# Index supply with three replica buffers and two staging buffers, and a reordered shift of batch 0, in a cross-attention and table-weight FFN kernel

## What is computed

```python
def attn(q, k, v):                  # 16 heads of 32
    p = softmax(einsum('bhqd,bhkd->bhqk', q, k) * HD ** -0.5)
    return einsum('bhqk,bhkd->bhqd', p, v)
q = head_norm(layernorm(x) @ Wq + bq)
k, v = head_norm(y[:, :-16] @ Wk + bk), y[:, :-16] @ Wv + bv
kd, vd = head_norm(y[:, -16:] @ Wkd + bkd), y[:, -16:] @ Wvd + bvd
x = x + (attn(q, k, v) + attn(q, kd, vd)) @ Wo + bo
gate, up, down = lut[gate_idx], lut[up_idx], lut[down_idx]   # 1376x512, 1376x512, 512x1376
n = layernorm(x)
x = x + (silu(n @ gate.T) * (n @ up.T)) @ down.T
```

## Time and profile before

| | us |
|---|---|
| median of three runs | 851.1 |
| profiled execution | 852.15 |
| its span | 850.0 |
| PE busy | 777.9 (92%) |
| DVE busy | 521.7 (61%) |
| ACT busy | 489.0 (58%) |
| POOL busy | 232.6 (27%) |

### The profile page before, as it was taken

How to read it: one execution, slowest core, us unless ns; L and a number is a source line. 1 busy time by engine, 2 the same in 40 slices (tenths; PEclk the granted TensorE clock), 3 DMA queues, 4 the chain that set the end, 5 groups by cost and what they waited for, 6 DMA issues and landing times.

```text
span 850.0 us, 14775 instructions
## 1 busy us (share of the span) xinstructions
PE 777.9 (92%) x5842; PEld 313.7 (37%) x5842; DVE 521.7 (61%) x1007; ACT 489.0 (58%) x993; POOL 232.6 (27%) x248
## 2 busy tenths in 40 slices
PE   3777666699999999999999999999999999999998
PEld 1332122222345333333454333324543332255445
DVE  7879899787685899321757993216579931053211
ACT  3577567677645788565357885652568856521100
POOL 6772210000057222100472222003732210013320
PEclk9987768799999999999999999999999999999999
DMA  7928844366521000122210001312100000000001
GB/s 242 263 96 245 241 142 110 82 159 155 137 53 35 1 1 1 51 62 50 69 46 1 1 1 34 79 38 75 27 1 1 1 26 26 26 25 1 0 13 38
DMA packets 72532, 56.50 MB, mean 66 GB/s; under 512 B 33232, under 2 KB 60624, under 8 KB 72464
## 3 DMA queue, kind: packets, MB, share of 16 engines
q1 hardware_dynamic: 72128, 55.31, 24.1%
q10 hardware_dynamic: 208, 0.26, 0.1%
q0 software_dynamic: 128, 0.00, 0.0%
HBM read 40.67 MB, written 8.45 MB: 58 GB/s over the span
## 4 chain that ended last, share of the span: by engine, by line
PE 67%; DVE 19%; ACT 4%; SPq 3%; DMA 2%; issue 2%; POOL 2%; DVEq 0%; POOLq 0%; ACTq 0%
PE ps L1339 49%; PE ps L1613 6%; DVE arena L890 5%; PE ps L1594 4%; DVE nmax L1145 3%; PE ps L1567 3%; DVE nmax L1146 3%; DMA arena<-idx 2%; PE ps L1390 2%; ACT ps L793 2%; SPq L368 2%; DVE nmax L1142 2%; DVE arena L897 2%; PE ps L1513 1%; PE ps L1600 1%
## 5 line engine op out<-in xcount | busy, mean ns | idle before, releaser
L1339 PE MATMUL ps<-arena,wf_hi 128*128 128x512 f16 (+2 forms) x736 | 211.1, 371 | 4.1 <-DVE arena L897 3.0
L793 ACT ACTIVATE ps<-ps,nmax 128x496 f32<-128x496 f32 x256 | 165.8, 649 | 26.9 <-DVE nmax L1145 26.9
L821 ACT ACTIVATE arena<-ps 128x1024 f32<-128x1024 f32 x128 | 124.2, 1024 | 72.7 <-PE ps L1600 72.6
L1339 PE MATMUL ps<-arena,wf_lo 128*128 128x512 f16 (+2 forms) x368 | 136.1, 370 | 0.0
L1339 PE MATMUL ps<-wf_hi,arena 128*128 128x512 f16 (+3 forms) x374 | 114.8, 368 | 0.0
L590 POOL TENSOR_TENSOR hrstd<-hvar,mhalf 128x16 f32<-128x16 f32 (+1 forms) x33 | 98.0, 2984 | 44.7 <-DVE hvar L994 44.5
L1339 PEld LDWEIGHTS ps<-arena,wf_hi 128*128 128x128 f16 (+1 forms) x736 | 69.4, 100 | 90.2 <-DVE arena L897 13.1
L1390 PE MATMUL ps<-arena,wf_lo 128*32 128x512 f16 (+1 forms) x1056 | 80.9, 444 | 22.4 <-ACT wf_lo L660 16.6
L890 DVE TENSOR_SCALAR arena<-arena,wf_lo 128x2048 f16<-128x2048 f16 (+1 forms) x132 | 89.8, 740 | 14.8 <-DMA arena<-idx 11.1
L566 POOL TENSOR_TENSOR xrstd<-xvar,mhalf 128x1 f32<-128x1 f32 x32 | 20.0, 624 | 249.7 <-DVE xvar L932 249.7
L1339 PE MATMUL ps<-wf_lo,arena 128*128 128x512 f16 (+3 forms) x187 | 68.5, 366 | 0.0
(11 more groups left out here) (137 smaller groups left out, 1060.4 us busy)
## 6 DMA issues: line engine op xcount, KB each, us to landing
arena<-idx SPq DMA_DIRECT2D x124, 128.0 KB, 2.9
arena<-in_x SPq DMA_DIRECT2D x32, 256.0 KB, 3.0
wf_lo<-in_idx SPq DMA_DIRECT2D x10, 512.0 KB, 6.4
idx<-wf_hi SPq DMA_DIRECT2D x10, 384.0 KB, 5.1
out<-arena SPq DMA_DIRECT2D x15, 256.0 KB, 2.1
wf_lo<-in_idx SPq DMA_DIRECT2D x11, 256.0 KB, 8.1
arena<-in_ctxT SPq DMA_DIRECT2D x4, 512.0 KB, 4.6
arena<-in_Wq SPq DMA_DIRECT2D x4, 256.0 KB, 5.8
```

Of the source, the lines that this page charges most:

```text
L793: last = act.activation(sc, sc, ACT.Exp, bias=nmax[:, 0, t, h:h + 1], accum_out=den[:, 0, t, h:h + 1])
L821: act.activation(probs[n_ % 2][:, 2 * p:2 * p + 2, :], ps[:, bank:bank + 2, :], ACT.Exp).then_inc(s["probs_set"], 1)
L1339: last = pe.matmul(dst, l, r, start=(first and i == 0), stop=(stop and i == len(todo) - 1))
```

## The change

- Replicas get three buffers (the third in `ctx_first`, free once the context is split), so `load_rep(c)` waits for `one_hot(c - 3)`. Staging buffers go from four to two.
- SP issues `load_rep(c)` first in each step c, then store k and load k + 2 at c = 2k - 1 only, so that blocks move until c = 19. Steps with x work move by one.
- POOL's cast of block k waits for the one-hots of 2k - 5 chunks where that is more than k - 1, and `lookup_out` waits only for the cast of the blocks whose staging it overwrites.
- Batch 0's shift: a quarter of `one_hot(15)` stays ahead of the extra keys' work, one goes ahead of the sum and two behind it; all four low halves of `Wo` come behind the copy (L1174). `look_up(15)` moves from the shift into the first slot of phase two, all later look-ups of phase two one slot on, and the last two (31 and 32) stand behind phase two.
- ACT's high half of `Wo` becomes four pieces in slots 4, 6, 8 and 10 of phase one.
- In phase two of batches 0 to 2, a tile's standardisation (L937) comes one slot later than its moments, and moments and split stand behind the slot's `one_hot` or feed-forward work.

```diff
@@ -31,7 +31,7 @@
...
 NJ, NR4 = 4, 4
-STAGES, EARLY = 4, 1
+STAGES, REPS = 2, 3
 QK_SCALE = float(HD) ** -0.5
@@ -61,7 +61,8 @@
...
 S_ONE = NU + 2
-S_SHIFT = S_ONE + NS
+S_SUM = S_ONE + NS
+S_SHIFT = S_SUM + 1
 S_TWO = S_SHIFT + 2
@@ -263,6 +264,7 @@
...
         ctx_first = cut(KC * S)
+        l_rep += [ctx_first.bitcast(F16)]
         ctx_dca = cut(KC * MD)
@@ -281,7 +283,8 @@
...
         i_at = c_at - STAGES * 2 * STEP
-        l_idx = [wf_lo[:, i_at + i * 2 * STEP:i_at + (i + 1) * 2 * STEP].bitcast(I32) for i in range(STAGES)]
+        idx_at = [i_at + (STAGES - 1 - i) * 2 * STEP for i in range(STAGES)]
+        l_idx = [wf_lo[:, at_:at_ + 2 * STEP].bitcast(I32) for at_ in idx_at]
         l_c = [wf_lo[:, c_at + i * P:c_at + (i + 1) * P].rearrange("p (q k) -> p q k", q=NJ) for i in range(2)]
@@ -360,12 +363,14 @@
...
                     sp.wait_ge(s[f"idx_out{c // 3}"], 16)
-                if c >= 2:
-                    sp.wait_ge(s["oh_set"], NJ * (c - 1))
+                if c >= REPS:
+                    sp.wait_ge(s["oh_set"], NJ * (c - REPS + 1))
+                elif c == REPS - 1:
+                    sp.wait_ge(s["cT_lo"], 1)
                 src = idx16[:, lo:hi].rearrange("(g k) n -> k g n", g=NR4)
                 for r in range(NR4):
-                    dst = l_rep[c % 2][r * 32:(r + 1) * 32, 0:NR4 * (hi - lo)].rearrange("p (g n) -> p g n", g=NR4)
-                    sp.dma_start(dst, src).then_inc(s[f"rep_in{c % 2}"], 16)
+                    dst = l_rep[c % REPS][r * 32:(r + 1) * 32, 0:NR4 * (hi - lo)].rearrange("p (g n) -> p g n", g=NR4)
+                    sp.dma_start(dst, src).then_inc(s[f"rep_in{c % REPS}"], 16)
 
@@ -389,8 +394,7 @@
...
                 load_idx(it)
-            for it in range(EARLY):
-                store_idx(it)
+            store_idx(0)
             load_rep(0)
@@ -407,20 +411,22 @@
...
 
-            next_x = {4: (0, 1), 21: (2,), 24: (3,)}
-            turn_x = {21: 0, 24: 1, 27: 2, 30: 3}
-            for c in range(2, NCH):
-                if EARLY + c - 2 < IT:
-                    store_idx(EARLY + c - 2)
-                if c == 2:
+            load_rep(2)
+            store_idx(1)
+            next_x = {4: (0, 1), 22: (2,), 25: (3,)}
+            turn_x = {22: 0, 25: 1, 28: 2, 31: 3}
+            for c in range(REPS, NCH):
+                load_rep(c)
+                if c == REPS:
                     dca_values((0, 0))
+                if c % 2 and (c + 1) // 2 < IT:
+                    store_idx((c + 1) // 2)
                 if c in turn_x:
...
                     load_x(t, tile_of(flat, xaddr(0, 1, t)), xs[t % 2])
-                load_rep(c)
 
@@ -533,7 +539,7 @@
...
                 elif it > 1:
-                    pool.wait_ge(s["oh_set"], NJ * (it - 1))
+                    pool.wait_ge(s["oh_set"], NJ * max(it - 1, 2 * it - 5))
                 pool.wait_ge(s[f"idx_in{it % STAGES}"], 32 * (it // STAGES + 1))
@@ -654,8 +660,9 @@
...
                 act.wait_ge(s["oh_used"], NJ * (c + 1))
-                if lo < i_at <= hi - 1 or (c == 0 and i_at == 0):
-                    act.wait_ge(s["idx_16"], IT)
+                for i, at_ in enumerate(idx_at):
+                    if lo < at_ + 2 * STEP and hi > at_:
+                        act.wait_ge(s["idx_16"], max(it + 1 for it in range(IT) if it % STAGES == i))
                 act.activation(wf_hi[:, lo:hi], ps[:, FB, 0:hi - lo], ACT.Copy)
@@ -839,15 +846,21 @@
...
             def prepare(slot):
-                if slot == S_ONE + 3:
+                if slot in (S_ONE + 4, S_ONE + 6, S_ONE + 8, S_ONE + 10):
+                    g = (slot - S_ONE) // 2 - 2
                     act.wait_ge(s["wo_in"], 16)
-                    act.activation(fl(wo[0]), st_o, ACT.Copy, scale=WS).then_inc(s["wo_hi"], 1)
-                for c in lookups_in(slot):
-                    if c:
-                        lookup_out(c - 1)
+                    act.activation(wo[0][:, g, :], st_o[:, g * D:(g + 1) * D], ACT.Copy, scale=WS).then_inc(s["wo_hi"], 1)
+                if S_ONE <= slot < S_SUM - 1:
+                    for c in lookups_in(slot):
+                        if c:
+                            lookup_out(c - 1)
+                elif slot >= S_SHIFT + 1:
+                    for c in lookups_in(slot):
+                        lookup_out(c - 2)
 
             core((0, 0), prepare, (0, 1), None)
-            lookup_out(NCH - 1)
+            for c in range(NCH - 2, NCH):
+                lookup_out(c)
 
@@ -877,17 +890,17 @@
...
 
-            def one_hot(c):
+            def one_hot(c, quarters=range(NJ)):
                 lo, hi = CHUNKS[c]
                 n_ = NR4 * (hi - lo)
-                dve.wait_ge(s[f"rep_in{c % 2}"], 16 * NR4 * (c // 2 + 1))
+                dve.wait_ge(s[f"rep_in{c % REPS}"], 16 * NR4 * (c // REPS + 1))
                 if c == 0:
...
                     dve.wait_ge(s["ps1"], T)
-                for q in range(NJ):
+                for q in quarters:
                     if c:
                         dve.wait_ge(s["oh_used"], NJ * (c - 1) + q + 1)
-                    dve.tensor_scalar(l_oh[q][:, 0:n_], l_rep[c % 2][:, 0:n_], l_j[:, q:q + 1], None, ALU.is_equal)\
+                    dve.tensor_scalar(l_oh[q][:, 0:n_], l_rep[c % REPS][:, 0:n_], l_j[:, q:q + 1], None, ALU.is_equal)\
                        .then_inc(s["oh_set"], 1)
@@ -1156,6 +1169,7 @@
...
                 dca_shift(T - 1)
+                between(S_SUM)
                 dca_sum(T - 1)
@@ -1182,12 +1196,14 @@
...
                         attn_lo(n_ // T - 1)
-                    if nxt is not None:
-                        if n_ in NORM_AT:
-                            norm(1, NORM_AT[n_], nxt)
-                        if n_ in TURN_AT:
-                            stage(1, TURN_AT[n_], nxt)
+                    if nxt is not None and n_ - 1 in NORM_AT:
+                        t = NORM_AT[n_ - 1]
+                        standardise(1, t, nxt, xs[t % 2], xs[t % 2])
                     between(S_TWO + n_)
+                    if nxt is not None and n_ in NORM_AT:
+                        moments(1, NORM_AT[n_], nxt, xs[NORM_AT[n_] % 2])
+                    if nxt is not None and n_ in TURN_AT:
+                        stage(1, TURN_AT[n_], nxt)
                 attn_lo(G - 1)
@@ -1290,12 +1306,16 @@
...
             def prepare(slot):
-                if slot in (S_SHIFT, S_SHIFT + 1):
-                    dve.wait_ge(s["wo_hi"], 1)
-                    for g in (0, 1) if slot == S_SHIFT else (2, 3):
+                if slot == S_SHIFT + 1:
+                    dve.wait_ge(s["wo_hi"], G)
+                    for g in range(G):
                         low(wo[1][:, g, :], st_o[:, g * D:(g + 1) * D], wo[0][:, g, :]).then_inc(s["wo_lo"], 1)
+                if slot == S_SUM:
+                    one_hot(NQ - 1, (1,))
+                if slot == S_SHIFT:
+                    one_hot(NQ - 1, (2, 3))
                 for c in lookups_in(slot):
-                    one_hot(c)
+                    one_hot(c, (0,) if c == NQ - 1 else range(NJ))
 
@@ -1627,10 +1647,13 @@
...
                 for c in lookups_in(slot):
-                    if c:
+                    if slot < S_SUM and c:
                         look_up(c - 1)
+                    elif slot >= S_TWO:
+                        look_up(c - 2)
 
             core((0, 0), prepare, (0, 1), None)
+            look_up(NCH - 2)
             look_up(NCH - 1)
```

4 lines of the change are left out of this document (2 added, 2 removed).

## The result

The changed kernel takes 836.02 us (median of 4 runs, 835.61 to 836.72), where the kernel before takes 850.7 us (848.22 to 851.44): a ratio of 0.9833, interval 0.9812 to 0.9855. The forecast was 837, with a range of 831 to 846. The profiled span fell from 850.0 to 834.3 us.

The account below looks back on a forecast made before the run. DVE was taken to bound phase one and PE phase two of batch 0; 852.15 - 7.3 - 4.5 - 4.0 + 1.4 = 837.75, on the runs' scale 836.7, said as 837, range 831 to 846.

Parts of the forecast that it names:

- Phase one: Batch 0, 60 to 151 us: replica, Wo and cast waits go, 8.3 us, less 1.0 kept back for PE's clock: 7.3.
- rival D: Casts throughout batch 0's DVE-bound stretch collide with DVE if blocks land late; three cost 4.4 us, 841; chance 0.03.
- the jam: Batch 0, 60 to 110 us: loading a block every step delays replicas; slower blocks and earlier loads remove all 4.7 us.
- The shift: Batch 0, from the last maxima to the second set of scores: reordering starts these about 4.5 us earlier; bounds 2.5 to 5.5.
- Phase two: Batch 0's PE-bound stretch up to the last value product: 61.5 us becomes 57.5, 4.0 less; bounds 0 to 5.5.
- Rival B: Batch 0's PE-bound stretch gains nothing: x work still touches on DVE, or SP's transposes delay replicas; 841; chance 0.13.
- The end: Behind batch 0's last value product, two look-ups instead of one: 5.6 us where 4.2 were, 1.4 us more.
- The allowances: Reserves held back from the gains: 1.0 us for PE's lower clock, 1.5 us for replicas and DVE in PE-bound slots.
- rival A: In batch 0, all reserves come back (1.0 + 1.5, and a bit around the logarithm): 834 us; chance 0.12.
- C: PE's lower clock makes PE the bound of batch 0's first stretch: 7 us lost, 844; chance 0.08.
- E: Stores and block loads on SP's queue delay replicas over 2 us in eight steps: 16 us lost, 853; chance 0.04.

Follow-up runs that it names:

- the repeat: The changed kernel measured again, unaltered, beside the other experiments: 836.01 us in the first group, 835.21 us in the third.
- the best experiment: Changed kernel with PE's wait for the last copy-outs and Wo's low half moved behind batch 1's first two products: 832.95 us.

## Why the prediction was right

- **Phase one**: 7.3 us predicted, 7.9 measured. All waits went, as said, and of the 1.0 us held back for the clock nothing was needed; the clock rose. Instead 1.7 us went to the collisions of rival D, which I had set at 0.03. D's condition (blocks that land late) was not what brought them: of the three casts that collide, two start on time, released by a one-hot. Of the six casts after 85 us three lie over an extra-key instruction. The held instruction ends 0.27 or 0.28 us after the end of its cast each time (85.76 + 1.47 = 87.23 and 86.72 + 0.79 = 87.51 for the first), and so do all 28 held instructions of the fourteen traces. The Trainium skill, SBUF — State Buffer, section "Who interferes with whom", describes one engine held for the whole instruction of the other; here 0.42 us became 0.79 and 1.37, and 0.42 again when the cast moved away. Without collisions phase one is 78.59 us (casts later), 9.5 less than before, where the terms added up to 8.3. So a gain that I had counted too small and a loss that I had left out nearly cancelled, which was luck.
- **Why replicas were late** was half right. I had put it down to the jam that blocks at every step make. With blocks at every step and 270 GB/s, three buffers had no wait; with two buffers, slow blocks and replicas first in SP's order phase one had none either. Each of the two cures alone is enough in phase one, and the slow blocks, beside three buffers, cost 1.1 us by their later casts. The number came out right because I had taken the whole wait off, whichever cured it.
- **The shift**: 4.5 predicted, 5.0 to the second scores. With its order undone the stretch is 15.67 us, as before, so the order is the cause. Of its 5.2 us against the repeat 3.8 are left at batch 1's first product, mostly because the end is longer with it. The half microsecond over the forecast is the look-up's: the one behind the first scores took 3.06 us, not the 3.60 that I had counted. The drain of about 1380 ns that the Trainium skill gives in ScalarE: Activation LUTs, "What ACT_TABLE_LOAD costs", isn't there: in the changed kernel the load ran from 142.87 for 1.28 us, the activation ahead of it ended at 142.86, and the next instruction of ACT started at 144.17.
- **Phase two**: 4.0 predicted with 1.5 held back; from the second scores to the end of the last value product are 207.90 - 151.33 = 56.6 us, where 61.5 were, so 4.9. From scores to scores thirteen slots take 3.70 us, one 4.3. Rival B is out. Its first reason (moments next to standardisation) cost nothing beside the lag. Its second (SP at a transpose while a replica is due) was real, as two buffers show with 4.18 us, and the third buffer covers it. What I didn't see is that buffer and order need each other: the buffer alone brings phase two from 61.5 us to 60.4, the new order with two buffers leaves it at 61.6, and both give 56.6. DVE's replica waits, 6.4 us before and 11.4 with two buffers, don't show this, since undisturbed slots take 3.70 us in both kernels and the stretch is as long; the larger sum took the place of other waits, and 4.18 of it lie behind phase two.
- **The end**: 1.4 us more predicted, 1.9 measured (gaps of 0.97 and 1.19, the look-up at 2.39 instead of 1.91 us). This was the one term against the change, and the best experiment takes 1.0 to 1.4 us of it back.
- The allowances together (1.0 and 1.5) were the distance to rival A. The measured 836.0 lies between the two. Rivals C and E stayed out: the clock didn't bound phase one, and no replica was late in a step with a block.

What stays open: how the 13 to 15 us of the whole split between buffer and order. Undoing one at a time gives 9.9 and 2.5 (and 1 for Wo), adding the buffer alone gives 3; the parts need each other, and no split of the sum holds for both directions. Which part of the order the buffer needs in phase two, the lag of the look-ups, the x work or the place of replicas on SP, isn't shown: with the buffer, undoing the lag cost 0.75 us and undoing the x work nothing.

## What to carry to other kernels

The sum of an engine's waits for one thing is not what curing them is worth. Take one cause away and another wait can fill its place, so a buffer and a better order are to be priced together, on the length of the stage (here 61.5 us, 60.4 and 61.6 with one of them, 56.6 with both). On a queue that issues other work too, what a buffer is worth shows in how late the issues come and not in bandwidth (here 3.0 us for the last chunk, at a share of 0.58). A change that spreads an engine's work over a longer time also spreads what that work collides with. And when the end of a stage is pulled in, look at what the next stage loads, and at what releases that load: work that you move later can hold it back.

## What the runs showed of the hardware

- A share of 0.96 of the DMA engines, 270 GB/s, made no engine wait for a replica that had two steps of time.
- In the jam one issue of a block load held SP for 3.50 us (before) and 2.90 (a block every step), where it takes 0.70 to 0.83 in the changed kernel.
- The look-up of 32 products behind the first scores took 2.79, 3.06 and 3.60 us in three profiles of one kernel, and 2.13 to 3.60 over all kernels, between its times at the upper clock (1.91) and the lower (3.60), though the transposes and scores ahead of it are the same and take the same time. What decides when the clock comes back there stays open; it moves the end by up to 0.8 us from run to run.
- Beside casts of the same kernel the three extra-key instructions took 0.79, 1.37 and 0.78 us in one profile, and 0.77, 0.79 and 1.53 in another. Each ended 0.27 or 0.28 us after its cast, so its length depends on tenths of a microsecond in its start.
